# Delta rule in a four-sublayer kernel: where the diagonal 32 x 32 blocks are gathered, transposed and spread

## The reference, cut to what matters

```python
A = jnp.where(strict_lower, -jnp.einsum('bhnck,bhnjk->bhncj', k_beta, k), 0.0)
for i in range(1, chunk):                       # chunk = 32
    row = A[..., i, :]
    A = A.at[..., i, :].set(row + jnp.einsum('bhnj,bhnjc->bhnc', row, A))
T = A + jnp.eye(chunk, dtype=A.dtype)
u = jnp.einsum('bhncj,bhnjd->bhncd', T, v)
w = jnp.einsum('bhncj,bhnjd->bhncd', T, k_beta)
# then a scan over the chunks: attn, u - w S, o, S + k^T u
```

## Time and profile before

| | us |
|---|---|
| runs before, three: lowest, median, highest | 1237.24, 1242.61, 1242.72 |
| the profiled execution's own time | 1243.85 |
| span of that execution, first to last instruction | 1242.2 |
| the stage that the change touches, in that span | 77.5 to 239.4 |
| busy in the span: TensorE, VectorE, ScalarE, GpSimd | 881.1, 743.5, 411.8, 103.0 |
| mean granted TensorE clock | 0.801 of full speed |

### The profile page before, as it was taken

How to read it: one execution, slowest core, us unless ns; L and a number is a source line. 1 busy time by engine, 2 the same in 40 slices (tenths; PEclk the granted TensorE clock), 3 DMA queues, 4 the chain that set the end, 5 groups by cost and what they waited for, 6 DMA issues and landing times. The chain is left out here.

```text
span 1242.2 us, 17736 instructions
## 1 busy us (share of the span) xinstructions
PE 881.1 (71%) x6628; PEld 748.9 (60%) x6628; DVE 743.5 (60%) x1601; ACT 411.8 (33%) x722; POOL 103.0 (8%) x61
## 2 busy tenths in 40 slices
PE   4957698809724002589999994799999995427984
PEld 2437698805422002478989883588888885226864
DVE  3259996494667997321526356526767764576375
ACT  2326252204301001143544431224555552205552
POOL 0021030000004781000000000000000002000000
PEclk9977588658766556689999996558999998668987
DMA  6001200210001000000000002000000000000000
GB/s 162 0 0 23 47 2 2 117 83 1 0 0 53 0 0 0 1 1 1 1 0 0 0 0 96 0 1 2 1 1 0 2 2 1 0 0 1 1 0 34
DMA packets 17799, 19.65 MB, mean 16 GB/s; under 512 B 16592, under 2 KB 16720, under 8 KB 16976
## 3 DMA queue, kind: packets, MB, share of 16 engines
q1 hardware_dynamic: 17744, 18.90, 4.9%
HBM read 17.76 MB, written 1.15 MB: 15 GB/s over the span
## 5 line engine op out<-in xcount | busy, mean ns | idle before, releaser
L1633 PEld LDWEIGHTS PS<-VXT,PT 128*128 128x128 f32 x1024 | 129.6, 205 | 17.5 <-issue 13.3
L1633 PE MATMUL PS<-VXT,PT 128*128 128x73 f32 (+1 forms) x1024 | 136.8, 290 | 4.0 <-ACT PT L1656 4.0
L1274 ACT ACTIVATE HID<-PS,PB 128x512 f32<-128x512 f32 x128 | 87.3, 689 | 100.9 <-PE PS L1247 100.8
L1743 DVE TENSOR_REDUCE MX<-PS 128x2 f32<-128x512 f32 x128 | 81.6, 685 | 64.0 <-PE PS L1598 63.5
L1254 PEld LDWEIGHTS PS<-PB,HID 128*128 128x128 f32 x1024 | 118.6, 192 | 2.2
L1254 PE MATMUL PS<-PB,HID 128*128 128x128 f32 x1024 | 118.8, 275 | 0.0
L1342 DVE SCALAR_TENSOR_TENSOR OB<-PS,MS,OB 128x128 f32 (+1 forms) x128 | 36.1, 345 | 129.8 <-PE PS L1254 129.8
L1656 ACT ACTIVATE PT<-PS 128x512 f32<-128x512 f32 x128 | 68.6, 596 | 54.1 <-PE PS L1603 54.1
L1595 PE MATMUL PS<-Q,KZ 32*128 32x256 f32 x512 | 84.8, 430 | 2.0 <-ACT KZ L1412 2.0
L1598 PE MATMUL PS<-KZ,Q 32*128 32x256 f32 x512 | 82.2, 464 | 4.9 <-DVEq L113 3.1
L273 PE MATMUL PS<-PB,NRM 128*128 128x128 f32 x80 | 17.9, 417 | 88.1 <-DVE NRM L257 52.5
(11 more groups left out here) (354 smaller groups left out, 1963.9 us busy)
## 6 DMA issues: line engine op xcount, KB each, us to landing
PB<-in_pb SPq DMA_DIRECT2D x1, 5016.0 KB, 16.2
PB<-in_pd SPq DMA_DIRECT2D x1, 2888.0 KB, 9.6
X<-in_x SPq DMA_DIRECT2D x2, 1024.0 KB, 4.8
X<-fir_rows SPq DMA_DIRECT2D x2, 1024.0 KB, 6.7
TR<-fir_rows SPq DMA_DIRECT2D x2, 1024.0 KB, 8.8
PA<-in_pa SPq DMA_DIRECT2D x1, 1731.0 KB, 8.6
PC<-in_pc SPq DMA_DIRECT2D x1, 1560.0 KB, 6.8
out_x<-X SPq DMA_DIRECT2D x2, 512.0 KB, 2.7
```

The lines of the kernel that those rows point to most:

```text
L1274: nc.scalar.activation(HID[:, e % 2, c, :], PS[:, n % 8, :], ACT.Relu, bias=pb("b1")[:, at:at + 1]).then_inc(moe_act, 1)
L1633: last = nc.tensor.matmul(PS[:, UM.bank(n), col:col + VX], PT[:, k % 4, c, f * P:(f + 1) * P], v, start=(c == 0), stop=(c == 1))
L1743: nc.vector.tensor_reduce(MX[:, :, k], PS[:, UP_.bank(n), :].rearrange("p (f q) -> p f q", f=2), AX.X, ALU.max, negate=True).then_inc(p_dv ...
```

## The change

Two buffers come in: `DG`, 128 x 1024 elements, and `TG`, the same size, a view of `KBT`. Before `invert(x)` the diagonal blocks are copied from `GR[x]` to `DG`: positions c = 0, 1 by GpSimd, c = 2, 3 by ScalarE, each copy 32 x 1024 elements. VectorE then makes one transpose of 128 x 1024 elements from `DG` to `S`, and after the steps one of 128 x 1024 from `S` to `TG`. From `TG` the inverses are copied to the diagonal of `TBD`, again c = 0, 1 by GpSimd and c = 2, 3 by ScalarE.

ScalarE's gather stands in its program right behind the last `low` result of the half, and its spread right before its take of the first `ll` result of the half, so for half 0 behind the `fir` and `fs` results, and for half 1 behind all results of half 0. GpSimd spreads half 0, waits for all four spreads of half 0 (`a2_tbd` 4), and only then gathers half 1. GpSimd's identity copies now wait for the gathers instead of VectorE's read.

```diff
 @block.gpsimd
                     for x in range(2):
-                        pool.wait_ge(a2_read, 4 * x + 4)
-                        for c in range(4):
+                        F.wait_taken(pool, ("low", x, 1, NH - 1))
+                        for c in range(2):
                             own = slice(SUB * c, SUB * c + SUB)
-                            if x or c:
-                                pool.wait_ge(a2_eye, 4 * x + c)
+                            nc.gpsimd.tensor_copy(DG[own, :, :], GR[x][own, :, own]).then_inc(a2_diag, 1)
+                        for c in (2, 3, 0, 1):
+                            own = slice(SUB * c, SUB * c + SUB)
+                            pool.wait_ge(a2_diag, 4 * x + 4)
+                            if x or c != 2:
+                                pool.wait_ge(a2_eye, 4 * x + (c + 2) % 4)
                             nc.gpsimd.tensor_copy(GR[x][own, :, own], ident[own, own].unsqueeze(1).to_broadcast(
                                 [SUB, NH * HALF, SUB])).then_inc(a2_eye, 1)
+                        if x:
+                            break
+                        pool.wait_ge(a2_eye, 4)
+                        pool.wait_ge(a2_inv, 1)
+                        for c in range(2):
+                            own = slice(SUB * c, SUB * c + SUB)
+                            nc.gpsimd.tensor_copy(TBD[own, :, own], TG[own, :, :]).then_inc(a2_tbd, 1)
+                        pool.wait_ge(a2_tbd, 4)
...
+                    pool.wait_ge(a2_masked, 2 * NH)
+                    pool.wait_ge(a2_inv, 2)
+                    F.wait_full(pool, ("ll", 0, HALF - 1))
+                    for c in range(2):
+                        own = slice(SUB * c, SUB * c + SUB)
+                        nc.gpsimd.tensor_copy(TBD[own, :, own], TG[own, :, :]).then_inc(a2_tbd, 1)
 @block.scalar
                             nc.scalar.activation(GR[x][:, at:at + 4, :], tile4(PS[:, bank_of[key], :]), ACT.Copy,
                                                  scale=-1.0).then_inc(a2_act, 1)
+                            if (q, h) == (1, NH - 1):
+                                F.wait_taken(act, key)
+                                if x:
+                                    act.wait_ge(a2_read, 1)
+                                for c in (2, 3):
+                                    own = slice(SUB * c, SUB * c + SUB)
+                                    copy(DG[own, :, :], GR[x][own, :, own]).then_inc(a2_diag, 1)
...
+                        elif key[0] == "ll" and key[2] == 0:
+                            x = key[1]
+                            act.wait_ge(a2_inv, x + 1)
+                            act.wait_ge(a2_zero, 2)
+                            if x:
+                                F.wait_full(act, ("ll", 0, HALF - 1))
+                            for c in (2, 3):
+                                own = slice(SUB * c, SUB * c + SUB)
+                                copy(TBD[own, :, own], TG[own, :, :]).then_inc(a2_tbd, 1)
+                            take(act, copy, key, a2_act)
 @block.vector, invert(x)
-                        F.wait_taken(dve, ("low", x, 1, NH - 1))
-                        if x:
-                            dve.wait_ge(a2_tbd, 4 * x)
-                        for c in range(4):
-                            own = slice(SUB * c, SUB * c + SUB)
-                            nc.vector.transpose(S[own, :, :], GR[x][own, :, own].rearrange("p u j -> p j u"))\
-                                .then_inc(a2_read, 1)
-                        dve.wait_ge(a2_read, 4 * x + 4)
+                        dve.wait_ge(a2_diag, 4 * x + 4)
+                        nc.vector.transpose(S, DG[:, :, :].rearrange("p u j -> p j u")).then_inc(a2_read, 1)
+                        dve.wait_ge(a2_read, x + 1)
...
                         if x:
-                            F.wait_full(dve, ("ll", x - 1, HALF - 1))
-                        dve.wait_ge(a2_zero, 2)
-                        for c in range(4):
-                            own = slice(SUB * c, SUB * c + SUB)
-                            nc.vector.transpose(TBD[own, :, own].rearrange("p u i -> p i u"),
-                                                S[own, :, :].rearrange("p j i -> p i j")).then_inc(a2_tbd, 1)
+                            dve.wait_ge(a2_tbd, 4 * x)
+                        F.wait_full(dve, ("low", 1, 1, NH - 1))
+                        nc.vector.transpose(TG.rearrange("p u i -> p i u"), S.rearrange("p j i -> p i j"))\
+                            .then_inc(a2_inv, 1)
+                        if x == 0:
+                            dve.wait_ge(a2_inv, 1)
```

More of the change, by code:

```diff
@@ L427, in build @@
             W1T = sbuf(s2, "W1T", [P, 4, P])
+            DG = sbuf(s2, "DG", [P, NH * HALF, SUB])
+            TG = KBT[:, :, :].rearrange("p t c -> p (t c)").rearrange("p (u i) -> p u i", i=SUB)
             FS = DEL[:, :, :].rearrange("p t c -> p (t c)").rearrange("p (b l) -> p b l", b=B)
@@ L442, in build @@
                 sem("a2_lower"), sem("a2_fs"), sem("a2_tbd"), sem("a2_read"), sem("a2_eye"))
+            a2_diag, a2_inv = sem("a2_diag"), sem("a2_inv")
             events, ring = [], itertools.count()
```

## The result

The changed kernel's median is 1252.97 us over 20 executions (1240.33 to 1255.48); the kernel before, beside it on the same chip, had 1244.41 (20 executions, 1236.66 to 1262.42). The ratio is 1.0065, 95% interval [1.0041, 1.0089]: slower by 0.65%, where 1238.4 us and "within 0.5%" were predicted, and above the range. The interval reaches down to 0.41%. Ratios leave out executions more than 1.5% above the fastest of their kernel: here four of before's twenty, 1255.75 us and above, and none of the changed kernel's, so this ratio leans against the change.

What follows compares the result with a forecast made beforehand. VectorE was taken to set the stage's end, TensorE waiting 10.11 and 4.18 us for it. Four ScalarE pairs against two removed waits gave 4.2 us off 1243.85, 1239.65 profiled, 1238.4 median; range 1232 to 1243.5 us.

Steps and rivals of the forecast that it cites:

- The wide transpose: VectorE, around each inversion: one 128-partition transpose lasts as long as one old quarter, 1.95 us gathering, 2.2 us spreading.
- rival of quarters in turn: VectorE's wide transpose does the quarters one by one: 12.8 us slower, 1255.4 us; chance 0.04.
- ScalarE's pair: ScalarE's two 32 x 1024 copies per gather or spread: 2.1 us, bounds about 1.2 and about 4.
- G: Time of one pair of ScalarE's 32 x 1024 copies, taken as 2.1 us.
- rival of slow copies: ScalarE's strided copies in the four pairs cost VectorE's prices: 1242 to 1247 us, slower; chance 0.08.
- GpSimd's pair: GpSimd's two copies per gather or spread: 2.1 us, up to 4.2; contention may hold the short filter 2.1 us.
- The new order: Both halves: long filter starts at 118.2 us, first `ll` at 151.45, VectorE idle some 12 us, second `ll` at 192.7.
- The clock rising earlier: TensorE at `fs` and `ll`: without the 10 us gap, upper clock saves another 6.8 to 8.8 us, 1234.8 us; chance 0.27.
- 4G − 12.6: Start of half 1's `ll`: four ScalarE pairs join the path, two waits leave it; 4.2 us earlier.
- Behind it nothing changes, and the later stages move along whole.: Layers behind the stage: they keep their times, so the 4.2 us gain reaches the end.
- The same lottery can take 2 us away: TensorE's clock level can cost 2 us, counted within the forecast's 1236.4 to 1240.4 us.
- All saving arrives: Whole stage: VectorE's 25.3 us less four hand-overs of 2.2 gives 16.5 us gain, 1226.1 us; chance 0.03.

Runs made afterwards that it cites:

- e12: Kernel before plus one unread VectorE product (1.75 us) right behind the stage: 1242.96 us, ratio 1.0008 [0.9973, 1.0042].
- e1: Changed kernel measured again without edit: 1243.55 us over 12 executions, recorded ratio 1.0056 to the kernel before; the profiled execution took 1233.04 us.
- e16: Changed kernel without edit, one execution, second trace sought of its upper group: 1236.40 us.
- changed, first: Profiled execution of the changed kernel's first measurement, no further edit: 1246.93 us, 3.1 more than the profiled execution of the kernel before.
- e13: Changed kernel plus one unread VectorE product (1.75 us) right behind the stage: 1241.32 us, ratio 0.9980 [0.9954, 1.0006] to the kernel before.
- e15: Changed kernel without edit, one execution, for a trace of its upper group: 1255.31 us.
- e17: Changed kernel plus three unread VectorE products (about 5.3 us) behind the stage: 1249.28 us, ratio 1.0024 [0.9988, 1.0061] to the kernel before.
- e9: Kernel before, ended behind the delta rule with its result written out and later layers left out: 246.32 us (243.78 to 247.51).
- cut programs: Kernel before and changed kernel, each ended behind the delta rule with later layers left out: 246.32 and 245.53 us.
- e4: Changed kernel with VectorE making ScalarE's second gather and both spreads, GpSimd's wait for half 0's spreads dropped: 1229.94 us, ratio 0.9922 to the kernel before; repeated, 1226.91.
- e5: Kernel before plus two identity products ahead of each of four pieces of the first substitution step, both halves: 1250.38 us, ratio 1.0061 [1.0027, 1.0096].
- e6: Changed kernel with VectorE's four transposes back in front of the steps, wide transpose and spreads kept behind: 1242.11 us, ratio 0.9993 to the kernel before.
- e3: Changed kernel with gathers and wide transpose kept before the steps, VectorE's four transposes back behind them: 1237.74 us, ratio 0.9979 to the kernel before.

## Why the prediction was wrong, point by point

- **The wide transpose** is one of the old durations: 1.97, 2.01, 1.95 and 1.96 us; taken were 1.95 and 2.2. The rival of quarters in turn is out.
- **ScalarE's pair**: G = 2.13 us, forecast 2.1. The rival of slow copies is out.
- **GpSimd's pair**: 2.12 us, and 5.13 beside the short filter; this spread passes the 4.2 that was the upper bound. The filter itself took 6.05 us against 4.74, 1.3 more, within the 2.1 allowed; both sides paid, GpSimd 3.0 us for its pair. VectorE was ready at 139.8 us, and `fs` ran without a wait.
- **The new order**: long filter at 118.69 us (118.2), its first quarter 7.01 us long where before's was 6.14, so that it ended at 146.2 (144.9), first `ll` at 152.37 (151.45), hole on VectorE of 14.77 us (some 12), `ll` of half 1 released by ScalarE at 194.25 (192.7). The steps took 24.7 us, not 26.5 (130.37 − 105.63, 135.71 − 109.19), as more of the identity copies fell under the transpose; that was off the path.
- **The clock rising earlier**: `fs` took 3.43 us for 16 and the first `ll` 9.04, the forms of the lower level. With the gap gone, `fs` stood right behind 27 us of solid filter at the granted clock 0.50, and still ran at it. The rival that the Trainium skill's page on the clock gate backed (TensorE: Matmul & The Clock Gate, § What's actually happening) did not come true at this place.
- **The first failed step: the sum 4G − 12.6, as one number.** It took `ll` of half 1 as put forward by 4.2 us. But in the kernel before, VectorE's inverse released that `ll` with 4.18 us of slack over TensorE, and this slack absorbed what half 0's products lost to the clock. The change takes it away: ScalarE's spread stands behind the take of the last output, so their clock is on the path. From the end of the last `low` of half 0 (VectorE's first gather; in the changed kernel the start of the wide transpose less its 2.28 us wait), in us:

```
                      to ll of half 1    to the next stage
before                     95.6              138.3
before, e12                96.7              136.7
changed, e1 and e16        90.7              131.1
changed, first             92.9              141.7
changed, e13               95.3              138.0
changed, e15               95.2              137.9
changed, e17               95.1              137.9
```

The four groups of output products of half 0, 0.98 us each in e1 and 1.75 in e15, are 3.1 us of the 4.5 between these two, and the pairs of products of q between them, 0.47 to 0.49 us a pair and 0.77 to 0.80, another 1.2; first e1, then e15:

```profile
188.05 0.98 PE L654 MATMUL PS<-Y,PB 128*128 128x32 f32 x8
191.87 9.69 PE L603 MATMUL PS<-PB,GR 128*128 128x128 f32 x64 [2.84 <-ACT PB L721]
```

```profile
194.02 1.75 PE L654 MATMUL PS<-Y,PB 128*128 128x32 f32 x8
198.62 8.95 PE L603 MATMUL PS<-PB,GR 128*128 128x128 f32 x64 [2.84 <-ACT PB L721]
```

In the kernel before the slack shows. In e9 two steps of half 0's substitution ran at the lower level (5.33 and 6.43 us against 2.98 and 5.70), and its `ll` of half 1 still started 95.6 us after that end. In e12 the outputs ran as slowly as in e15 (four times 1.75) and cost 1.1 us, until TensorE came last itself; first e9, then e12:

```profile
198.84 10.26 PE L582 MATMUL PS<-PB,GR 128*128 128x128 f32 x64 [1.60 <-DVE PB L779]
200.14 9.87 PE L582 MATMUL PS<-PB,GR 128*128 128x128 f32 x64
```

So the forecast gain of 4.2 us is 4.9 us against before's profile where the outputs keep the upper level, and 0.3 to 0.5 where they don't (1.4 to 1.6 against e12, whose outputs were as slow). The hand-overs were right, and the cover was misjudged. The cut programs' medians, 0.8 us apart, agree.
- **The second failed step, which took it out of the range: "Behind it nothing changes, and the later stages move along whole."** The traces of e15, e13 and e17 show that the layers behind took up to 10 us more or less for a start a few microseconds apart, by the clock levels that they were granted. "The same lottery can take 2 us away" named the cause with a fifth of its size. The changed kernel has lost the group below 1239 us almost wholly (2 of 34 executions, before 33 of 136) and has half of its executions above 1252 (17 of 34, before 36 of 136).
- **"All saving arrives"** (1226.1 us) was refused by ScalarE's order, as the forecast said; e4, which takes ScalarE out of it, measured 1229.94 and 1226.91.

What stays open: why the layers behind meet the lower level in one execution and not in another, since the start alone doesn't decide it, and so which groups a kernel will get. The table shows where and how much, for single executions. That the groups of e13 and of the changed kernel differ by the same mechanism in every execution is argued from these, not shown. Other amounts of delay than one and three products were not tried, nor another place for ScalarE's spread in its own order, nor e3 or the delay in a second series.

## What to carry to other kernels

An engine that is waited for with slack is also a shield: it keeps the next engine's variations off the path. When you move its work, ask what the new releaser stands behind, and sum up for both clock levels of that. And in a program like this one a gain of a few microseconds in an early stage is worth only what the later stages' clock leaves of it: end the program behind the stage to price the stage, and delay the rest by an instruction that nobody waits for to see whether a difference of the whole belongs to the change at all. Here three of ScalarE's four pairs of copies belonged on the engine that had fallen idle.

## What the runs showed of the hardware

- A VectorE transpose of 128 x 1024 elements took 1.95 to 2.01 us, and one of 32 x 1024 in the kernel before 1.93 to 1.97 us in the gather's view and 2.17 to 2.30 in the spread's.
- The same program's executions form groups some 7 us apart or more (before: about 1237, 1244 and 1260 us), and added work changes which of them occur: of the changed kernel's executions 17 of 34 lay at 1252 to 1258, with 1.75 us of work none of 12, and with three times as much one of 12, with eight at 1248.6 to 1251.7.
- A stretch of 32 us in a later layer (770 to 802 us) lost 5.9 to 6.0 us to the lower clock level in five of sixteen traces and next to nothing in the rest, and two traces that reached it 0.1 us apart (e5, e6) fell on either side.
- GpSimd's copy of 32 x 1024 took 1.06 us in the gathers and 2.57 in the spread beside the short filter; beside its copies VectorE's steps of 184 elements took 1.15 us in place of 0.35 (e3).
